# Making the ternary weights of the last layer inside an earlier stage of a two-layer decoder

## The chip, the cores and the metric

The kernel runs on one core of a Trainium2 chip. The metric is the device time of one execution in microseconds (us), measured from outside the program; a profiled execution also has a span, from its first to its last instruction. Engines are named as in the profile: PE (TensorE matmuls), PEld (its weight loads), DVE (VectorE), ACT (ScalarE), POOL (GpSimd), SP (SyncE, which here only issues DMAs); SPq and POOLq are DMAs issued from those two engines.

## The reference

Input x is [4, 512, 512]: 2048 tokens of 512. Six blocks follow, each `x = layernorm(x + block(x))`: an 8-wide-head attention, a cross attention on features, a mixture of experts, a causal attention with rotary angles, a cross attention with axial rotary angles, and a gated feed-forward net with ternary weights. Two of them matter here.

- Mixture of experts: eight experts with hidden widths 256 to 1024, the best two for each token, on a latent of 256; a shared expert and a core matrix beside them.
- The ternary net. Its weights are 2048x512, 2048x512 and 512x2048 (4 MB each in float32), and each is quantised with one scale that needs the mean of all its magnitudes first:

```python
def _quant_weight(w):
    scale = jnp.mean(jnp.abs(w)) + EPS
    wq = jnp.clip(jnp.round(w / scale), -1.0, 1.0)
    return (wq, scale)
def _qlinear(x, w):            # activations are rounded to 8 bits with a scale per row
    wq, ws = _quant_weight(w)
    xq, xs = _quant_act(x)
    return jnp.einsum('bsi,oi->bso', xq, wq) * xs * ws
gate = silu(_qlinear(x, w_gate)); up = _qlinear(x, w_up); out = _qlinear(gate * up, w_down)
```

The weights depend on no activation, so they can be made at any time. The net multiplies by their transposes, so that each 128x128 block is also turned.

## The kernel before

The program runs stage after stage; the token array `m.x_tok` stays in SBUF. Each stage is a block in which every engine has its own instruction list, written out in the order of the Python loops; semaphores join the lists, and an engine that waits holds back all that stands behind in its list. All engines meet at the end of a block.

**The experts' items** (`mixture_of_experts`, L629). Tokens are sorted by expert into 24 tiles of 256 tokens, and the work is cut into `ITEMS` = 79 items, each one slice of 256 hidden columns of one expert on one tile. For item i the lists hold:

- SP (L741 to L779): two DMAs of the item's weights, 257 and 256 KB (`load_item`, three slots `item`, so three items ahead); for the first items the rows of a token tile (`load_rows`, 256 KB); every fourth item one `store_tile` (L758), which waits until DVE has added that tile's last item.
- PE (L943): `turn_rows(i + 4)` while there are tiles, `hidden(i + 1)` (8 matmuls, L924), `output(i)` (8 matmuls, L935). The result of `output` goes to one of four banks (`mm`), which DVE empties.
- ACT: the gelu of the hidden columns (L1022) and a copy of the next token tile (L1011).
- DVE (L1213 to L1220): `keep_turned(i + 4)` while there are tiles, then one add of the bank to the accumulator `acc` (L1220).
- POOL: nothing during the items. Its list has the scatter of the token rows, 24 memsets and four adds to x, then the wait `pool.wait_ge(s.stored, SPARE * 16)`, and the gathers that follow the last item.

`w.core` (8 KB a partition) and `w.down` (4 KB) are weights of this stage that are last read before the items.

**The ternary weights** (`ternary_weights`, L2307) are the first block of the last stage, and the token loop (`ternary_ffn`) is its second. SP loads 12 pieces of 1 MB. ACT adds up magnitudes piece by piece (L2367); PE sums them over the partitions (L2418); DVE makes the scale (L2385 to L2389) and then, for each piece, three `tensor_scalar` passes over 128x2048: scale and round (L2394), subtract and cap at 1 (L2400), cap at -1 (L2402). PE turns the blocks, four 128x128 transposes to a bank, four banks to a piece (192 transposes, `turn_tile`, L117), and ACT and DVE copy every other bank to `tf_gate`, `tf_up`, `tf_down` (L2378, L2406). ACT's sums of weight i + 1 are interleaved with the turning of weight i. The order within DVE's list is `for c in range(PARTS + 1)`: quantise piece c, then copy the odd banks of piece c - 1.

Of the kernel before, what the change touches and what calls it, by code (L numbers as in the profile page):

```python
# [21 lines left out]
BF16 = mybir.dt.bfloat16  # L22
# [11 lines left out]
LN_EPS = 1e-5  # L34

# [524 lines left out]
class Packed:  # L560

    def __init__(self, nc, ctx):
        self.items = nc.dram_tensor("moe_items", (PAIR0[EXPERTS], P, PACKED), F32, kind="Internal").ap()
        self.sorted = nc.dram_tensor("moe_sorted", (TILES * TOKENS, LATENT), F32, kind="Internal").ap()
        self.mixed = nc.dram_tensor("moe_mixed", (SPARE * TOKENS, LATENT), F32, kind="Internal").ap()
        self.items_in, self.cleared = ctx.enter_context(nc.semaphore("moe_items_in")), ctx.enter_context(nc.semaphore("moe_cleared"))
# [61 lines left out]
def mixture_of_experts(nc, m, w, packed, a):  # L629
# [10 lines left out]
    LATER = 2  # L640
    EARLY, PAD = 4, T // 2 + 1
    hc_at = numbered([key for b in range(B) for key in [("x", b, j) for j in range(NT)] + [("rows", b - 1, h) for h in range(HALVES) if b > 0]]
                     + [("rows", B - 1, h) for h in range(HALVES)] + [("gates", b) for b in range(B)]
                     + [("turn", n) for n in range(TILES)] + [("sums", t) for t in range(T)])
# [7 lines left out]
    with ExitStack() as ctx:  # L652
# [46 lines left out]
        s.returned_in = [sem(f"returned_in_{i}") for i in range(RETURNED)]  # L699
        s.x_now_ready, s.returned_used = sem("x_now_ready"), sem("returned_used")  # L700
# [81 lines left out]
        def _(pe):  # L782
# [251 lines left out]
        def _(dve):  # L1034
# [173 lines left out]

            dve.wait_ge(s.which_ready, 1)
            for n in range(AHEAD):  # L1210
                keep_turned(n)
            for i in range(ITEMS):
# [7 lines left out]
                dve.tensor_tensor(to, bank(("item", i)), to, ALU.add).then_inc(free(("item", i)), 1)  # L1220

# [36 lines left out]
        def _(pool):  # L1258
# [30 lines left out]
            for b in range(B):  # L1289
                x = m.x_tok[:, b * NT:(b + 1) * NT, :]  # L1290
                pool.tensor_tensor(x, x, w.up_b[:].unsqueeze(1).to_broadcast([P, NT, D]), ALU.add).then_inc(s.x_biased, 1)
            pool.wait_ge(s.stored, SPARE * 16)
# [1008 lines left out]
INNER = 2048  # L2301
KI = INNER // P
QUANT_EPS = 1e-5
ROUND_INT = 1.5 * 2.0 ** 23

def ternary_weights(nc, m, w, w_gate, w_up, w_down):  # L2307

    WEIGHTS, PARTS = 3, 4
    FREE = D * INNER // P
    PIECE = FREE // PARTS
    SLOTS = 6
    LOADS = 3
    with ExitStack() as ctx:
        sb, sem = allocator(nc, ctx, "tw")
        raw = [sb(f"raw{i}", [P, FREE]) for i in range(WEIGHTS)]  # L2320
        quant = sb("quant", [P, SLOTS, PIECE], BF16)
        sums, ones, total, inv = sb("sums", [P, 3, PARTS]), sb("ones", [P, P]), sb("total", [P, 3]), sb("inv", [P, 3])
        ident_b, spare = sb("ident_b", [P, P], BF16), sb("spare", [P, PIECE], BF16)
        loaded = [sem(f"loaded{i}") for i in range(LOADS)]
        made, ident_made, summed, added, scaled, rounded = (sem(n) for n in ("made", "ident_made", "summed", "added", "scaled", "rounded"))
        full = [sem("even_full"), sem("odd_full")]
        free = [sem("even_free"), sem("odd_free")]
        TILES = D * INNER // (P * 4 * P)
        BANKS = TILES // PARTS
        block = ctx.enter_context(nc.Block())  # L2330

        def turned(i, n):

            if i < 2:
# [4 lines left out]
        def piece(i, c):  # L2339
            return raw[i][:, c * PIECE:(c + 1) * PIECE]  # L2340

        def wait_loaded(engine, i, c):
            q = i * PARTS + c
            engine.wait_ge(loaded[q % LOADS], q // LOADS * 16 + 16)

        @block.sync
        def _(sp):
            for i, source in enumerate((w_gate, w_up, w_down)):
                rows = P * PIECE // source.shape[1]
                for c in range(PARTS):  # L2350
                    if i * PARTS + c >= LOADS:
                        q = i * PARTS + c - LOADS
                        wait_loaded(sp, q // PARTS, q % PARTS)
                    sp.dma_start(piece(i, c).rearrange("p (o n) -> p o n", n=source.shape[1]),
                                 source[c * rows:(c + 1) * rows, :].rearrange("(o p) n -> p o n", p=P)) \
# [326 lines left out]
```

## Time and profile before

| | |
|---|---|
| median of 3 runs | 3102.58 us (3102.41 to 3107.42) |
| the profiled execution's own time | 3105.17 us |
| its span | 3103.4 us |
| busy share of the span: PE, DVE, ACT, POOL | 90%, 59%, 45%, 13% |
| experts' items, by DVE's first and last add | 830.1 to 1106.2 us |
| ternary weights block, first DMA issue to last copy | 2789.9 to 2859.6 us |
| DMA | 147.54 MB, mean 48 GB/s |

### The profile page before, as it was taken

What the parts mean: (1) busy time and instruction counts of PE and PEld (TensorE: products, weight loads), DVE (VectorE), ACT (ScalarE), POOL (GpSimd) and SP (SyncE); (2) the same over time, 40 slices, a digit from 0 to 9 for tenths busy, and PEclk for the clock granted to TensorE, in tenths of its full rate; (3) what the DMA queues carried; (4) which work ended last, traced back from release to release, by engine and by line L of the source; (5) the groups of instructions that cost most, each with busy time, mean ns of one, the idle gap of its engine ahead of it and who ended that gap; (6) DMA issues with size and microseconds to landing.
All of it is one profiled execution on the core that took longest, in us unless ns stands there. A gap on an engine that the chain in (4) does not pass through costs nothing. (4 is left out here: it accounts for less than half of the span.)

```text
span 3103.4 us, 40349 instructions
## 1 busy us (share of the span) xinstructions
PE 2781.8 (90%) x12377; PEld 1644.4 (53%) x12400; DVE 1839.6 (59%) x3505; ACT 1394.6 (45%) x2964; POOL 398.8 (13%) x437
## 2 busy tenths in 40 slices
PE   8999996889999976998998998996999999983887
PEld 4455453344688845655655655654555454433333
DVE  5666563524222155756756756753777777746776
ACT  4454442121133412543542642542667676745544
POOL 0310003003300041102102102102010101000010
PEclk9999998999899998999999999998999999995999
DMA  3390007002366634000000000001000000004000
GB/s 129 49 100 14 14 0 247 29 1 75 94 193 172 171 102 156 1 1 15 1 1 15 1 1 14 1 1 55 8 2 9 2 5 2 2 8 157 7 20 27
DMA packets 74599, 147.54 MB, mean 48 GB/s; under 512 B 11136, under 2 KB 27537, under 8 KB 71985
## 3 DMA queue, kind: packets, MB, share of 16 engines
q1 hardware_dynamic: 62976, 111.53, 11.2%
q0 software_dynamic: 11440, 33.77, 5.8%
q8 instruction: 91, 1.49, 0.2%
q14 instruction: 92, 0.75, 0.1%
HBM read 112.50 MB, written 31.22 MB: 46 GB/s over the span
## 5 line engine op out<-in xcount | busy, mean ns | idle before, releaser
L2207 DVE TENSOR_REDUCE x_neg_max<-bank 128x1 f32<-128x512 f32 x512 | 327.2, 684 | 96.1 <-PE bank L2052 95.5
L2159 ACT ACTIVATE x_weights<-bank 128x512 f32<-128x512 f32 x512 | 279.1, 600 | 127.1 <-PE bank L2063 122.3
L1507 PE MATMUL bank<-a_wo,a_att_cols 128*128 128x512 f32 x512 | 226.9, 594 | 7.8 <-DVE a_q_cols L1607 4.1
L1557 ACT ACTIVATE a_probs<-bank,a_neg_max 128x128 f32<-128x128 f32 (+3 forms) x256 | 138.4, 540 | 192.5 <-DVE a_neg_max L1655 192.2
L117 PE MATMUL bank<-all_ident,a_probs 128*128 128x128 f32 x1216 | 197.0, 275 | 16.3 <-DMA a_probs<-all_x_tok 16.3
L117 PEld LDWEIGHTS bank<-all_ident,a_probs 128*128 128x128 f32 x1216 | 155.3, 142 | 104.4 <-issue 52.5
L1549 ACT COPY a_probs_t<-bank 128x128 f32<-128x128 f32 (+3 forms) x256 | 108.7, 424 | 193.7 <-PE bank L117 193.7
L1220 DVE TENSOR_TENSOR moe_acc<-bank,moe_acc 128x512 f32 x79 | 54.6, 692 | 214.0 <-PE bank L935 214.0
L1482 PE MATMUL bank<-a_k_cols,a_q_cols 128*128 128x128 f32 (+3 forms) x512 | 176.8, 434 | 0.0
L1448 PE MATMUL bank<-a_x_high,a_w_high 128*128 128x512 f32 x320 | 137.3, 429 | 38.6 <-DVE a_q_cols L1607 12.9
L1686 POOL TENSOR_TENSOR a_w_low<-a_wqkv,a_w_high 128x512 fp32r<-128x512 f32 x64 | 81.4, 1272 | 591.0 <-ACT a_w_high L1520 591.0
L1507 PEld LDWEIGHTS bank<-a_wo,a_att_cols 128*128 128x128 f32 x512 | 94.2, 190 | 113.4 <-issue 106.0
L924 PE MATMUL bank<-moe_gh_cols,moe_item 128*128 128x256 f32 x632 | 151.2, 382 | 0.4 <-issue 0.4
L935 PE MATMUL bank<-moe_item,moe_wide 128*128 128x256 f32 x632 | 149.4, 379 | 0.0
L1494 PE MATMUL bank<-a_probs_t,a_v_rows 128*128 128x512 f32 (+3 forms) x512 | 148.6, 433 | 0.0
L1563 ACT ACTIVATE a_probs<-a_probs,a_inv_sum 128x128 f32<-128x128 f32 (+3 forms) x256 | 144.8, 566 | 2.5 <-DVE a_inv_sum L1660 2.5
L1022 ACT ACTIVATE moe_wide<-bank,moe_item 128x256 f32<-128x256 f32 x158 | 66.3, 470 | 166.5 <-PE bank L924 166.5
L2052 PE MATMUL bank<-x_k_cols,x_q_cols 64*128 64x512 f32 x512 | 136.4, 496 | 3.5 <-DVE x_neg_max L2207 3.4
L1629 DVE TENSOR_TENSOR all_x_tok<-bank,all_x_tok 128x512 f32 (+1 forms) x64 | 44.2, 691 | 158.6 <-PE bank L1507 158.6
L1655 DVE TENSOR_REDUCE a_neg_max<-bank 128x1 f32<-128x128 f32 (+3 forms) x256 | 125.7, 491 | 20.9 <-issue 2.6
L2085 PE MATMUL bank<-x_weights,x_v_rows 128*17 128x512 f32 x1024 | 134.5, 598 | 0.0
L2063 PE MATMUL bank<-x_q_cols,x_k_cols 64*128 64x512 f32 x512 | 127.6, 415 | 3.2 <-ACT x_weights L2159 2.8
(402 smaller groups left out, 5714.1 us busy)
## 6 DMA issues: line engine op xcount, KB each, us to landing
moe_item<-moe_items SPq DMA_DIRECT2D x79, 257.0 KB, 3.0
moe_item<-moe_items SPq DMA_DIRECT2D x79, 256.0 KB, 3.2
moe_items<-in_L_ffn_e_w POOLq DMA_DIRECT2D x40, 256.0 KB, 35.3
moe_sorted<-x_zeros POOLq DMA_DIRECT2D x1, 6144.0 KB, 22.8
moe_x_cols<-moe_sorted SPq DMA_DIRECT2D x24, 256.0 KB, 3.6
moe_mixed<-moe_acc SPq DMA_DIRECT2D x23, 256.0 KB, 3.3
all_x_tok<-in_x SPq DMA_DIRECT2D x1, 4096.0 KB, 17.7
x_x_rows<-all_x_tok SPq DMA_DIRECT2D x4, 1024.0 KB, 9.1
```

What stands on the lines that cost most here:

```text
L117: last = pe.transpose(bank[:, c * P:(c + 1) * P], rows[:, c * P:(c + 1) * P], ident)
L924: last = pe.matmul(bank(("hidden", i))[:, c * TOKENS:(c + 1) * TOKENS], weight[:, k, c * P:(c + 1) * P], x_now[:, i % 2, k * TOKENS:(k + 1 ...
L935: last = pe.matmul(bank(("item", i))[:, j * LATENT:(j + 1) * LATENT], hid[:, i % 2, c * TOKENS + j * P:c * TOKENS + (j + 1) * P], weight[: ...
L1448: last = pe.matmul(mm[g % 2], weight[:, p % 2, k, :], x[:, k, :], start=n == 0, stop=n == 3 * KD - 1)
L1482: pe.matmul(sc[n % 4][:, 0:t], q_cols[:, h % 2, j * P:t], k_cols[:, h // GROUP, 0:t], start=True, stop=True).then_inc(s.sc.full, 1)
L1494: last = pe.matmul(mm[g % 2][:, c * P:], v_rows[:, c, kv * HD1:(kv + 1) * HD1], probs_t[:, n % 2, c, c * P:], start=c == 0, stop=c == NT - 1)
L1507: last = pe.matmul(mm[g % 2], att_cols[:, h % HALF_HEADS, j * P:(j + 1) * P], wo[:, h, :], start=h == first, stop=h == end - 1)
L1557: act.activation(probs[:, n % SLOTS, 0:t], sc[n % 4][:, 0:t], ACT.Exp, bias=neg_max[:, n:n + 1], accum_out=row_sum[:, n:n + 1]).then_inc(s ...
L1563: act.activation(probs[:, i % SLOTS, 0:t1], probs[:, i % SLOTS, 0:t1], ACT.Copy, scale=inv_sum[:, i:i + 1]).then_inc(s.probs_ready, 1)
L2052: pe.matmul(score_banks[slot % 3], q_cols[rows, u % 2, pair, j * P:(j + 1) * P], k_cols[rows, u % 2, pair, :], start=True, stop=True).then ...
L2159: act.activation(weights[:, chunk % 2, k, :], weight_banks[slot % 2], ACT.Exp).then_inc(s.weight.free, 1)
L2207: dve.tensor_reduce(neg_max[:, g % 2, j, h:h + 1], score_banks[slot % 3], AX.X, ALU.max, negate=True) \
```

## The change

The three weights are made ternary during items 12 to 63 and written to a DRAM tensor `packed.ternary` in bf16; the last stage loads that tensor (6 MB instead of 12) and only turns it. Each weight is cut into eight pieces of 128x1024 (512 KB in float32, 256 KB in bf16), 24 in all, in two buffers over `w.core` (raw) and two over `w.down` (ternary).

- Items 12 to 35: after each item's add, DVE sums the magnitudes of one piece, with one `tensor_reduce`.
- Item 38: PE sums over the partitions, one small matmul. Item 39: DVE makes the three scales.
- Items 40 to 63: after each item's add, DVE makes one piece ternary, in the same three passes as before. The pieces are loaded from DRAM a second time.
- POOL issues all of these DMAs, in one loop that stands ahead of its wait for `s.stored`: 24 loads for the sums, and 24 loads and 24 stores for the ternary round. Load q + 2 waits until DVE is done with piece q.
- The last stage's first block has 12 loads of 512 KB (six ahead), 192 transposes over all eight banks, and the copies, shared out between ACT and DVE as before. No sum, no scale and no quantising pass is left in it.

```diff
@@ mixture_of_experts
+    EIGHTHS_ALL = WEIGHTS * EIGHTHS
+    SUM_AT, SCALE_AT = 12, 12 + EIGHTHS_ALL + 2
+    QUANT_AT = SCALE_AT + 2
...
+        raw = w.core[:].rearrange("p k n -> p (k n)").rearrange("p (i n) -> p i n", i=2)
+        ternary = w.down[:].rearrange("p k n -> p (k n)").bitcast(BF16).rearrange("p (i n) -> p i n", i=2)
...
@@ tensor
+                if i == SCALE_AT:
+                    pe.wait_ge(s.abs_summed, EIGHTHS_ALL)
+                    pe.wait_ge(*room("scale"))
+                    pe.matmul(bank("scale")[:, 0:EIGHTHS_ALL], ones[:], abs_sum[:].rearrange("p i g -> p (i g)"),
+                              start=True, stop=True).then_inc(full("scale"), 1)
@@ vector
+            def add_magnitudes(q):
+                dve.wait_ge(s.raw_in[q % 2], (q // 2 + 1) * 16)
+                dve.tensor_reduce(abs_sum[:, q // EIGHTHS, q % EIGHTHS:q % EIGHTHS + 1], raw[:, q % 2, :], AX.X, ALU.add,
+                                  apply_absolute_value=True).then_inc(s.abs_summed, 1)
...
+            def make_ternary(q):
+                slot, i = q % 2, q // EIGHTHS
+                dve.wait_ge(s.raw_in[slot], (EIGHTHS_ALL // 2 + q // 2 + 1) * 16)
+                dve.tensor_scalar(raw[:, slot, :], raw[:, slot, :], inv_scale[:, i:i + 1], ROUND_INT, ALU.mult, ALU.add)
+                dve.drain()
+                if q >= 2:
+                    dve.wait_ge(s.ternary_out[slot], q // 2 * 16)
+                dve.tensor_scalar(ternary[:, slot, :], raw[:, slot, :], ROUND_INT, 1.0, ALU.subtract, ALU.min)
+                dve.drain()
+                dve.tensor_scalar(ternary[:, slot, :], ternary[:, slot, :], -1.0, None, ALU.max).then_inc(s.ternary_ready, 1)
...
                 dve.tensor_tensor(to, bank(("item", i)), to, ALU.add).then_inc(free(("item", i)), 1)
+                if SUM_AT <= i < SUM_AT + EIGHTHS_ALL:
+                    add_magnitudes(i - SUM_AT)
+                if i == SCALE_AT + 1:
+                    weight_scales()
+                if QUANT_AT <= i < QUANT_AT + EIGHTHS_ALL:
+                    make_ternary(i - QUANT_AT)
@@ gpsimd
+            for n in range(2 * EIGHTHS_ALL + 2):
+                q = n - 2
+                if 0 <= q < EIGHTHS_ALL:
+                    pool.wait_ge(s.abs_summed, q + 1)
+                elif q >= EIGHTHS_ALL:
+                    q -= EIGHTHS_ALL
+                    pool.wait_ge(s.ternary_ready, q + 1)
+                    pool.dma_start(packed.ternary[q // EIGHTHS, q % EIGHTHS], ternary[:, q % 2, :]).then_inc(s.ternary_out[q % 2], 16)
+                if n < 2 * EIGHTHS_ALL:
+                    load_raw(n)
...
             pool.wait_ge(s.stored, SPARE * 16)
@@ ternary_weights
-            for i, source in enumerate((w_gate, w_up, w_down)):
...
+            for q in range(PIECES):
+                if q >= LOADS:
+                    sp.wait_ge(loaded[q % LOADS], q // LOADS * 16)
+                i, c = divmod(q, PARTS)
+                sp.dma_start(quant[:, q, :].rearrange("p (g n) -> p g n", g=2),
+                             packed.ternary[i, 2 * c:2 * c + 2].rearrange("g p n -> p g n")).then_inc(loaded[q % LOADS], 16)
...
+            for n in range(0, WEIGHTS * TILES, 2):
+                act.wait_ge(full[0], n // 2 + 1)
+                act.copy(turned(n), blocks_of(bank(n), 4)).then_inc(free[0], 1)
...
+            for n in range(1, WEIGHTS * TILES, 2):
+                dve.wait_ge(full[1], n // 2 + 1)
+                dve.tensor_copy(turned(n), blocks_of(bank(n), 4)).then_inc(free[1], 1)
...
+            for n in range(WEIGHTS * TILES):
+                q, part = divmod(n, BANKS)
+                if part == 0:
+                    pe.wait_ge(loaded[q % LOADS], q // LOADS * 16 + 16)
+                pe.wait_ge(free[n % 2], n // 2 + 1)
+                turn_tile(pe, bank(n), quant[:, q, part * 4 * P:(part + 1) * 4 * P], ident_b[:], 4).then_inc(full[n % 2], 1)
```

The order of DVE's list in the later items, before: `moe_which` holds each item's tile number, and `moe_acc<-bank,moe_acc` is the add.

```order
497 L1215 TENSOR_LOAD moe_which
498 L1215 ISA x2
499 L1220 ISA
500 L1220 TENSOR_TENSOR moe_acc<-bank,moe_acc 128x512
501 L1215 TENSOR_LOAD moe_which
```

And in the changed kernel at items 40 and 41: `ew_core` is the raw piece, `ew_down` the ternary one.

```order
546 L1266 TENSOR_TENSOR moe_acc<-bank,moe_acc 128x512
547 L1247 TENSOR_SCALAR ew_core<-ew_core,moe_inv_scale 128x1024
548 L1251 TENSOR_SCALAR ew_down<-ew_core 128x1024
549 L1253 TENSOR_SCALAR ew_down<-ew_down 128x1024
550 L1261 TENSOR_LOAD moe_which
551 L1261 ISA x2
552 L1266 ISA
553 L1266 TENSOR_TENSOR moe_acc<-bank,moe_acc 128x512
```

Three passes, and the wait for the piece ahead of the first, now stand between one item's add and the next one's.

POOL's list from the adds to x to the gathers, before:

```order
178 L1288 MEMSET moe_acc 128x512 x24
179 L1291 TENSOR_TENSOR all_x_tok<-all_x_tok,ew_up_b 128x2048 x4
180 L1299 DMA moe_x_cols<-moe_mixed,moe_index 128x256 x18
```

And in the changed kernel, its beginning (the last two rows then repeat):

```order
179 L1343 TENSOR_TENSOR all_x_tok<-all_x_tok,ew_up_b 128x2048 x4
180 L1354 DMA ew_core<-in_L_ffn_w_gate 128x2x512 x8
181 L1354 DMA ew_core<-in_L_ffn_w_up 128x2x512 x8
182 L1354 DMA ew_core<-in_L_ffn_w_down 128x1024 x8
183 L1354 DMA ew_core<-in_L_ffn_w_gate 128x2x512 x2
184 L1363 DMA ternary<-ew_down 128x1024
185 L1354 DMA ew_core<-in_L_ffn_w_gate 128x2x512
```

The 72 new DMAs stand between the adds to x and the gathers; in the second round a store and a load follow one another.

## Rows read from the trace of the kernel before

**Rows 1.** The page, busy time of each engine over the span.
```profile
PE 2781.8 (90%) x12377; PEld 1644.4 (53%) x12400; DVE 1839.6 (59%) x3505; ACT 1394.6 (45%) x2964; POOL 398.8 (13%) x437
```

**Rows 2.** Windows: us, busy of PE, PEld, DVE, ACT, POOL, PE clock, DMA share, GB/s.
```profile
870.00:890.00 20.00, 20.00 (x104) 17.61 (x103) 6.75 (x11) 6.78 (x15) 0.00 (x0) 1.00 0.74 216
950.00:970.00 20.00, 20.00 (x95) 17.58 (x94) 3.75 (x6) 8.32 (x18) 0.00 (x0) 1.00 0.64 184
2800.00:2810.00 10.00, 0.56 (x2) 0.50 (x2) 3.14 (x6) 6.20 (x8) 0.00 (x0) 0.50 1.05 390
2830.00:2840.00 10.00, 4.41 (x39) 3.86 (x39) 9.48 (x14) 8.46 (x11) 0.00 (x0) 0.50 0.00 1
```

**Rows 3.** DVE's add in the items, by its line: duration, idle before it by releaser.
```profile
L1220 DVE TENSOR_TENSOR moe_acc<-bank,moe_acc x79: 690/692/693, 830.1 to 1106.2; 128x512 f32 x79
  PE bank L935: 214.0, 79
```

**Rows 4.** Timeline of one item's add: start, us, engine, line, names, count, idle before.
```profile
935.16 0.69 DVE L1220 TENSOR_TENSOR moe_acc<-bank,moe_acc 128x512 f32 x1 [2.77 <-PE bank L935]
```

**Rows 5.** Timeline of the ternary block, its start, one piece, its end.
```profile
2789.93 5.88 SPq L2354 DMA_DIRECT2D tw_raw<-in_L_ffn_w_gate  x4
...
2795.52 1.91 ACT L2367 ACTIVATE tw_spare<-tw_raw 128x2048 bf16<-128x2048 f32 x1 [24.48 <-DMA tw_raw<-in_L_ffn_w_gate]
...
2828.78 0.58 ACT L2378 COPY tf_up<-bank 128x512 bf16<-128x512 bf16 x1 [2.88 <-PE bank L117]
...
2829.64 0.58 ACT L2378 COPY tf_up<-bank 128x512 bf16<-128x512 bf16 x1 [0.27 <-PE bank L117]
...
2859.13 0.42 DVE L2406 COPY tf_down<-bank 128x512 bf16<-128x512 bf16 x1 [0.43 <-PE bank L117]
```

**Rows 6.** Groups by line, 2740 to 2880: busy us, mean ns, idle before.
```profile
L2367 ACT ACTIVATE tw_spare<-tw_raw 128x2048 bf16<-128x2048 f32 x12 | 22.9, 1910 | 27.9 <-DMA tw_raw<-in_L_ffn_w_gate 26.7 <-DMA tw_raw<-in_L_ffn_w_up 0.7
L2394 DVE TENSOR_SCALAR tw_raw<-tw_raw,tw_inv 128x2048 f32<-128x2048 f32 x12 | 15.4, 1279 | 0.3
L2400 DVE TENSOR_SCALAR tw_quant<-tw_raw 128x2048 bf16<-128x2048 f32 x12 | 14.7, 1227 | 1.3
L2402 DVE TENSOR_SCALAR tw_quant<-tw_quant 128x2048 bf16<-128x2048 bf16 x12 | 8.3, 694 | 0.9
L2604 DVE TENSOR_REDUCE tf_top_h<-tf_inner 128x1 f32<-128x2048 f32 x1 | 2.3, 2287 | 0.1
L2588 DVE TENSOR_SCALAR tf_shifted_x<-all_x_tok,tf_inv_x 128x512 f32<-128x512 f32 x3 | 1.5, 486 | 0.2
```

**Rows 7.** DMA issues: count, KB each, median us from issue to landing.
```profile
moe_item<-moe_items SPq DMA_DIRECT2D x79, 257.0 KB, 3.0
...
ew_core<-in_L_ffn_core_w POOLq DMA_DIRECT2D x1, 1024.0 KB, 11.7
...
ew_down<-in_L_ffn_down_w POOLq DMA_DIRECT2D x1, 512.0 KB, 4.6
...
moe_sorted<-moe_acc,moe_index POOLq DMA_INDIRECT x32, 2.4
```

**Rows 8.** Timelines of POOL and DVE (129 on), columns as in rows 4.
```profile
128.96 0.98 POOL L579 DMA_DIRECT2D moe_items<-in_L_ffn_e_w  x1
129.04 2.02 DVE L97 TENSOR_SCALAR all_x_tok<-all_x_tok,a_ln_mean_var,a_ln_rstd  x4 [1.15 <-POOL a_ln_rstd L104]
...
131.42 0.69 POOL L579 DMA_DIRECT2D moe_items<-in_L_ffn_e_w  x1
```

**Rows 9.** Timeline of PE at the items' start, turning rows, then matmuls.
```profile
817.40 4.00 PE L913 MATMUL bank<-all_ident,moe_x_cols 128*128 128x128 f32 x16
...
821.78 3.75 PE L924 MATMUL bank<-moe_gh_cols,moe_item 128*128 128x256 f32 x8 [0.38 <-issue]
```

**Rows 10.** Windows there, columns as in rows 2.
```profile
821.00:822.00 1.00, 0.62 (x3) 0.25 (x3) 0.84 (x2) 0.67 (x2) 0.00 (x0) 0.50 0.84 273
...
826.00:827.00 1.00, 1.00 (x7) 0.90 (x6) 0.69 (x1) 0.99 (x2) 0.00 (x0) 1.00 0.19 20
```

More of the change, by code:

```diff
@@ L643, in mixture_of_experts @@
                      + [("rows", B - 1, h) for h in range(HALVES)] + [("gates", b) for b in range(B)]
-                     + [("turn", n) for n in range(TILES)] + [("sums", t) for t in range(T)])
+                     + [("turn", n) for n in range(TILES)] + ["scale"] + [("sums", t) for t in range(T)])
     lg_at = numbered([(kind, b) for b in range(B) for kind in ("router", "logits")] + ["rank", "const", "sum"]
@@ L2337, in turned, with bank @@
             return w.down[:, 4 * q:4 * q + 4, o * P:(o + 1) * P]
[L2339 to L2344, printed above, removed]
+        def bank(n):
+            return m.banks[n % 8].bitcast(BF16)
         @block.sync
         def _(sp):
-            for i, source in enumerate((w_gate, w_up, w_down)):
[L2349 to L2355, printed above, removed]
-                      .then_inc(loaded[(i * PARTS + c) % LOADS], 16)
@@ L2363, in _ @@
         def _(act):
-            def add_up(i, c):
-                wait_loaded(act, i, c)
-                act.drain()
-                act.activation(spare[:], piece(i, c), ACT.Abs, accum_out=sums[:, i, c:c + 1]).then_inc(summed, 1)
-            for c in range(PARTS):
-                add_up(0, c)
-            for i in range(WEIGHTS):
-                for c in range(PARTS):
-                    if i + 1 < WEIGHTS:
-                        add_up(i + 1, c)
-                    for n in range(c * BANKS, (c + 1) * BANKS, 2):
-                        g = i * TILES // 2 + n // 2
-                        act.wait_ge(full[0], g + 1)
-                        act.copy(turned(i, n), blocks_of(m.banks[2 + g % 2].bitcast(BF16), 4)).then_inc(free[0], 1)
+            for n in range(0, WEIGHTS * TILES, 2):
+                act.wait_ge(full[0], n // 2 + 1)
+                act.copy(turned(n), blocks_of(bank(n), 4)).then_inc(free[0], 1)
@@ L2408, in _ @@
+            for n in range(1, WEIGHTS * TILES, 2):
+                dve.wait_ge(full[1], n // 2 + 1)
+                dve.tensor_copy(turned(n), blocks_of(bank(n), 4)).then_inc(free[1], 1)
         @block.tensor
         def _(pe):
[L2410 to L2412 removed]
+            pe.sem_inc(free[0], 4)
+            pe.sem_inc(free[1], 4)
             pe.wait_ge(ident_made, 1)
[L2414 to L2426 removed]
```

110 lines of the change are left out of this document (45 added, 65 removed).

## The prediction

> **What bounds the kernel now.** I read the page first: PE is busy for 90% of the span, so work taken from any other engine pays only where PE waits [rows 1]. The table of windows shows two stretches that the change touches and that are opposites. In the items PE is busy for all of 20 us out of 20 at the full clock, while DVE works for 3.75 to 6.75 us and POOL not at all; the DMA share is 0.64 to 0.74. In the ternary block PE is busy for 0.56 and 4.41 us out of 10, at a granted clock of 0.50, and the busiest engine is first the DMA (390 GB/s, share 1.05), then DVE (9.48 of 10) [rows 2]. The reader is to see in the first an engine that nothing may delay, and in the second a block that DMA and DVE set.
>
> Next the line of DVE's add: 79 adds of 692 ns, with 214.0 us of idle time before them, all ended by PE. DVE waits for PE, never the reverse [rows 3]. One of them shows the item's length: 2.77 us idle and 0.69 of add, 3.46 us [rows 4]. That is the cover for the moved work.
>
> Last the ternary block itself: first DMA issue at 2789.93, first sum at 2795.52, last copy from 2859.13 to 2859.55 [rows 5]. It lasts 69.6 us, and nothing else runs beside it.
>
> **The ternary block, what goes and what is left.** The 12 sums on ACT (22.9 us) and DVE's three passes over 12 pieces (15.4 + 14.7 + 8.3 = 38.4 us) go [rows 6]. Left are 12 loads of 0.5 MB, 192 transposes and 48 copies; what is late next is found by the rate of each.
> - DMA: 524 KB at 390 GB/s is 1.34 us a piece [rows 2]. The first 1 MB piece was used 5.6 us after its issue, of which 2.7 is transfer [rows 5]; a half piece saves 1.3. So the first piece is there at 2795.5 - 1.3 = 2794.2, the last at 2794.2 + 11 x 1.34 = 2808.9.
> - PE at the clock of this block: ACT copies every other bank, and two of its copies with PE as releaser start 0.86 us apart (2828.78, 2829.64), so a bank takes 0.43 us and a piece of four banks 1.72 [rows 5].
> - ACT: two copies a piece, 0.58 us each, 1.2 us. DVE's take 0.42 each [rows 5].
>
> PE is the slowest of them: 12 x 1.72 = 20.6 us from 2794.2 is 2814.8, and the last copy ends 0.7 later, 2815.5. Against 2859.55 that saves 44.0 us. It rests on the half clock. PE has nothing to turn before the first piece is there, in either kernel, so it starts at 0.50. Would gapless transposes lift it? At the items' start 16 transposes ran for 4.00 us without a gap (817.40) and the clock was still 0.50 after them; then eight matmuls ran 3.75 us from 821.78, and at 826 it was 1.00 [rows 9, 10]. I therefore leave it at half.
>
> The Trainium skill says the same in "TensorE: Matmul & The Clock Gate", Part 4: the full level does not engage for transposes, since they don't count as a busy PE in the same way. Its Part 1 would have them counted as sustained activity like matmuls; which of the two holds for twenty microseconds of them, no run here shows yet.
>
> With the full clock from 2801 on, DMA would be the slowest: last piece at 2808.9, turned and copied about 2 us later, 2811. That saves 48.5 us, and is the upper end of this term. The lower end is 42, if the half-size loads reach only nine tenths of the rate.
>
> **The items, what is added to DVE.** The shapes are new (128x1024), the operations not. A pass over 2048 takes 1279 ns and over 512 takes 486 [rows 6], so over 1024 by the line through both 750, of which 220 is there at any size. With half of the slope part and this fixed part the three passes take 0.75 + 0.72 + 0.46 = 1.9 us, with drains 2.0. The sum over 2048 takes 2287 ns (`tf_top_h`) [rows 6], over 1024 about 1.25. Against 2.77 us of idle time per item both fit, with 0.77 us left in the ternary round and 1.5 in the sums' round; in the first 20 items DVE also copies turned tiles, and is busy for 6.75 us in 20 instead of 3.75 [rows 2]: the 13 us left in 20 hold five sums of 1.25. So the arithmetic costs nothing as long as the piece is there when DVE comes to it. The matmul for the scales and its wait: 0.3 us; the three tiny DVE operations 0.5 us, hidden.
>
> **The items, the wait that is added.** DVE now waits for a DMA between two adds. Behind that wait stands the next item's add, behind the add the bank that PE needs four items later, and SP's `store_tile`, behind which the next item's weights stand. A slot is reloaded only when DVE is done with it, so two items must hold one whole round trip. For the ternary round: 2.0 (passes) + 0.1 + 0.7 (POOL issues the store) + landing of the load. For the sums' round: 1.25 + 0.1 + landing. The trace has no load of this kind in this place, so I bound the landing from both sides. An indirect DMA of 128 KB from POOL lands 2.4 us after its issue [rows 7]; less 0.34 of transfer that is 2.06 fixed, plus 1.34 for our size 3.4. The one load of our size from POOL, `ew_down`, took 4.6 [rows 7]. Beside it come the item loads, which hold the queues: the share of 0.64 [rows 2] leaves 0.36, and a transfer of 1.34 beside half-busy engines takes 2.0 to 2.7, so 4.1 to 6.0 in all. An upper end comes from a load that queued behind others, `ew_core` with 11.7 [rows 7].
> - Sums' round: 1.35 + 4.1 to 6.0 = 5.5 to 7.4 us for two items of at least 6.9. No cost, up to 5 us; I take 1.
> - Ternary round: 2.8 + 4.1 to 6.0 = 6.9 to 8.8 us, 3.45 to 4.4 an item against 3.46. Times 24 items: 0 to 23 us. DVE may fall behind PE by one to two items before PE (four banks) or SP's store feels it, which absorbs some 5 us. So 0 to 18; I take 7, for 3.95 us an item.
>
> By bytes the ternary round wants 513 + 512 + 256 KB an item and a fourth of 256 for the tile stores, 1.38 MB in 3.46 us or 398 GB/s. The highest rate in these rows is 390 [rows 2]. That is why I don't take zero.
>
> The item loads themselves (3.0 us to landing [rows 7]) are issued up to three items, 10.4 us, ahead of use, so they can double without reaching PE. 72 more issues on POOL at 0.7 us [rows 8] lie in its idle stretch, and the loop ends near item 66, before the wait for `s.stored` opens.
>
> One rule speaks against the change. What the rows show: with four DVE passes from SBUF to SBUF running beside it (129.04), POOL's issue took 0.98 us, and 0.69 two us later [rows 8]. So an overlap costs POOL about 0.3 us, and I have it within the range.
>
> The Trainium skill, "SBUF — State Buffer", on the trap that DVE blocks DMA, says that a DVE operation in a two-port mode locks GpSimd out, so that no descriptors of a POOL DMA are written until it ends. By that rule each of the two issues per item could wait for a whole pass of 0.75 us, 1.5 us in the round trip; the sum would then lose 24 x 0.75 = 18 us more, and still end faster than before.
>
> **The sum.** Profiled execution 3105.2 - 44.0 (block) + 7 (ternary round) + 1 (sums' round) + 0.3 (scale matmul) = 3069.5. The median of the runs shown stands 2.6 us below that execution (3102.6 against 3105.2), so I forecast 3067 us.
>
> **Rivals.**
> - A, the clock rises in the turning block. For: PE has no gaps there, unlike before, when it was busy for 4.41 us in 10 [rows 2]. Against: rows 9 and 10 as read above. The block then saves 48.5, and the time is 3062.5; if besides the round trips are all hidden, 3054.
> - B, the ternary round is bound by its round trip much more than I take, 4.6 us an item, through the port lock or both streams at 398 GB/s: 24 x 1.14 - 5 = 22, so 15 more than forecast, 3082. For: the byte count; against: PE-side slack and the share of 0.64.
> - C, slower than before: POOL's loads queue as `ew_core` did, because each load stands behind a store and behind the item loads in every DMA engine. With a landing of 11.7 the ternary round takes (2.8 + 11.7) / 2 = 7.25 us an item and the sums' round 6.5, against 3.46 and about 3.6. Less 5 each, that is 86 + 65 = 151 us, and the time is 3102.6 - 44 + 151 = 3210. It decides from a landing of 7.3 us on, where both rounds together lose the 44 (ternary 5.05, sums 4.3 an item: 38 + 17 - 10 = 45). Against: `ew_core` stood behind 1 MB of earlier loads of its own queue; here at most one store of 256 KB does.
> - D, the change doesn't do what it says: some pass or sum would still run in the last block. The listing of instructions shows none, so I give it nothing.
>
> **How the numbers follow.** Forecast with its own range of 3058 to 3077: 0.68. A with hidden round trips, below 3058: 0.10. B: 0.16. C: 0.06. The range holds the time 8 times in 10 when it reaches from 3054 to 3083: it leaves out C and a few in a hundred on either side. A measurement of this kernel tells 0.2% (6 us) from no change. Faster needs less than 3096: the forecast, A, B and the mild end of C, 0.95. Same 0.02, slower 0.03.
>
> **What the new profile would show.** Right if: the items' adds span 276 + 5 to 15 us; in items 40 to 63 DVE's first pass has idle time before it with the load as releaser, and in items 12 to 35 the sum has next to none; PE idle in the items is a few us; the last block has 24 + 24 copies, a clock of 0.50 and a length of 24 to 28 us. The size of the turning term is wrong if the clock there is 1.00. Wrong in the main if PE's idle time in the items passes 44 us, or if the first piece of the last block lands much later than 4.3 us after its issue.

## The result, and the profile after

The changed kernel takes 3089.09 us (median of 6 runs, 3077.00 to 3098.03), the kernel before 3103.74 beside it: a ratio of 0.9951, 95% interval 0.9931 to 0.9971. So 15 us came where 36 were forecast. The profiled execution took 3098.03 us, the slowest of the six, with a span of 3096.3.

The span by stages, read from DVE's adds (items), SP's first DMA (later blocks) and POOL's first instruction (token loop), in the profiled executions:

| stage | before | after | difference | forecast |
|---|---|---|---|---|
| up to the first add | 830.1 | 832.3 | +2.2 | 0 |
| items 0 to 12 | 46.7 | 46.7 | 0.0 | 0 |
| items 12 to 36 (sums) | 86.0 | 89.9 | +3.9 | +1 |
| items 36 to 40 (scales) | 13.8 | 14.9 | +1.0 | +0.3 |
| items 40 to 64 (ternary) | 82.9 | 111.0 | +28.1 | +7 with the next row |
| items 64 to 78 | 46.7 | 43.6 | -3.0 | |
| last add to fourth block | 70.2 | 68.9 | -1.3 | 0 |
| fourth block (causal attention) | 949.8 | 952.1 | +2.4 | 0 |
| fifth block (rotary cross attention) | 663.8 | 669.6 | +5.8 | 0 |
| ternary weights block | 69.9 | 21.7 | -48.2 | -44.0 |
| token loop | 243.6 | 245.7 | +2.1 | 0 |
| sum | 3103.4 | 3096.3 | -7.1 | -35.7 |

First the page, in answer to [rows 1]:

```profile
PE 2794.7 (90%) x12396; PEld 1649.4 (53%) x12396; DVE 1878.6 (61%) x3559; ACT 1371.0 (44%) x2940; POOL 443.8 (14%) x508
```

DVE is busier, not idler: moving work doesn't remove it, and each weight is now cut into smaller passes.

The items 40 to 64 as windows (the columns of [rows 2]), a stretch of before for comparison, then after:

```profile
962.80:1045.70 82.90, 82.90 (x385) 72.91 (x384) 16.60 (x24) 33.27 (x72) 0.00 (x0) 1.00 0.61 172
```
```profile
984.40:1095.40 111.00, 94.48 (x413) 80.25 (x412) 61.91 (x97) 35.72 (x78) 27.53 (x46) 0.95 0.91 299
```

PE, busy for every microsecond before, is idle for 16.5 of 111, and its clock is at 0.95 instead of 1.00. What DVE does there, by line (columns as in [rows 6]), answers to [rows 3]:

```profile
L1247 DVE TENSOR_SCALAR ew_core<-ew_core,moe_inv_scale 128x1024 f32<-128x1024 f32 x24 | 19.0, 790 | 32.9 <-DMA ew_core<-in_L_ffn_w_up 12.1 <-DMA ew_core<-in_L_ffn_w_down 11.4 <-DMA ew_core<-in_L_ffn_w_gate 9.4
L1266 DVE TENSOR_TENSOR moe_acc<-bank,moe_acc 128x512 f32 x25 | 17.3, 692 | 14.7 <-issue 10.9 <-PE bank L950 3.8
L1251 DVE TENSOR_SCALAR ew_down<-ew_core 128x1024 bf16<-128x1024 f32 x24 | 16.9, 703 | 1.8
L1253 DVE TENSOR_SCALAR ew_down<-ew_down 128x1024 bf16<-128x1024 bf16 x24 | 10.3, 427 | 1.8
```

Before, every add waited for PE. Now the add waits for PE for 3.8 us, and the first pass waits for the raw piece for 32.9. PE's own waits there have one row (wait, total, times, longest):

```profile
PE bank L939 <- DMA moe_item<-moe_items: 16.5, 7, 6.0
```

It names a DMA of item weights, which lands 1.6 us later than before at the median; but SP issues it behind a `store_tile` that waits for DVE. The landings in that stretch, after, answer to [rows 7]:

```profile
moe_item<-moe_items SPq DMA_DIRECT2D x26, 257.0 KB, 4.6
ternary<-ew_down POOLq DMA_DIRECT2D x24, 256.0 KB, 4.4
ew_core<-in_L_ffn_w_up POOLq DMA_DIRECT2D x8, 512.0 KB, 6.1
ew_core<-in_L_ffn_w_down POOLq DMA_DIRECT2D x8, 512.0 KB, 6.2
ew_core<-in_L_ffn_w_gate POOLq DMA_DIRECT2D x6, 512.0 KB, 7.0
```

The ternary block (against [rows 5]) and its windows:

```profile
2828.96 6.91 SPq L2412 DMA_DIRECT2D tw_quant<-ternary  x9
2832.64 3.57 PE L123 MATMUL bank<-tw_ident_b,tw_quant 128*128 128x128 bf16 x32 [8.99 <-DMA tw_quant<-ternary]
...
2848.81 1.07 PE L123 MATMUL bank<-tw_ident_b,tw_quant 128*128 128x128 bf16 x16 [0.22 <-DMA tw_quant<-ternary]
...
2849.47 0.87 DVE L2426 COPY tf_down<-bank 128x512 bf16<-128x512 bf16 x2 [0.41 <-PE bank L123]
```
```profile
2834.00:2839.00 5.00, 5.00 (x54) 5.00 (x53) 2.50 (x7) 3.55 (x7) 0.00 (x0) 0.55 1.04 389
2839.00:2844.00 5.00, 3.71 (x61) 3.20 (x59) 3.13 (x8) 3.77 (x8) 0.00 (x0) 1.00 1.05 387
```

PE starts at 0.50 and turns without a gap; the clock is 0.55 in the first window shown and 1.00 in the second. A piece of 16 transposes then takes 1.07 us, and PE waits for DMA, whose share is 1.05 at 387 GB/s: rival A's picture.

### The profile page after: what moved, and what is told of

Same layout as the page of the kernel before. It is cut to its first block and busy times, and to the rows that moved or that the text cites. A ratio compares the mean times of both kernels' runs of the same rounds, so it can differ in the third digit from the quotient of the medians.

```text
span 3096.3 us, 40464 instructions
## 1 busy us (share of the span) xinstructions
PE 2794.7 (90%) x12396; PEld 1649.4 (53%) x12396; DVE 1878.6 (61%) x3559; ACT 1371.0 (44%) x2940; POOL 443.8 (14%) x508
## 3 DMA queue, kind: packets, MB, share of 16 engines
q8 instruction: 91, 1.49, 0.2%
## 5 line engine op out<-in xcount | busy, mean ns | idle before, releaser
L939 PE MATMUL bank<-moe_gh_cols,moe_item 128*128 128x256 f32 x632 | 157.9, 395 | 20.2 <-DMA moe_item<-moe_items 19.7
L939 PEld LDWEIGHTS bank<-moe_gh_cols,moe_item 128*128 128x128 f32 x632 | 121.5, 197 | 41.6 <-DMA moe_item<-moe_items 24.9
L950 PEld LDWEIGHTS bank<-moe_item,moe_wide 128*128 128x128 f32 x632 | 121.9, 193 | 17.3 <-issue 0.3
```

The source lines that it names most:

```text
L939: last = pe.matmul(bank(("hidden", i))[:, c * TOKENS:(c + 1) * TOKENS], weight[:, k, c * P:(c + 1) * P], x_now[:, i % 2, k * TOKENS:(k + 1 ...
L950: last = pe.matmul(bank(("item", i))[:, j * LATENT:(j + 1) * LATENT], hid[:, i % 2, c * TOKENS + j * P:c * TOKENS + (j + 1) * P], weight[: ...
```

## The experiments

Kernels of one group ran on one chip, beside runs of the kernel before. The groups differ by 1.2% (medians of before 3103 to 3139 us; 0.4% between the second and the fourth, which have the same chip number), so ratios are compared across groups, and stage times from profiles: before has 86.0 us in items 12 to 36 and 82.9 in 40 to 64 in every profile of it. Theory 1 is the round trip through two buffers, theory 2 the bytes, theory 3 DVE's own work and POOL's descriptors beside it.

**First group** (before 3134.3 us). Four raw buffers in the ternary round, the two new ones over `x_cols`:

```diff
-                dve.wait_ge(s.raw_in[slot], (EIGHTHS_ALL // 2 + q // 2 + 1) * 16)
+                piece = raw_again(q)          # (raw, raw, more, more)[q % 4]
+                dve.wait_ge(s.again_in[q % 4], ...)
```

> Four buffers for the raw pieces of the ternary round instead of two (the two more lie over the token rows' buffers, free by then); bytes, passes and their places in DVE's list are as in the changed kernel. Theory 1, the round trip of a buffer: DVE's 32.9 us of waits for raw loads in the ternary round come from two items having to hold 2.0 us of passes, two issues and a landing of 6 us or more; with four items for it they go, items 40 to 64 take 83 to 87 us instead of 111, and the time is 3060 to 3066. Theory 2, the DMA engines are full: 1.38 MB an item at the 300 GB/s that were delivered is 4.5 us an item whatever the buffers, the round stays at 105 to 111 us, and the time at 3084 to 3090.

The load ahead of the store in POOL's list, released by the second pass:

```diff
+                        pool.wait_ge(s.raw_free, q + 1)
+                        load_raw(n)
                     pool.wait_ge(s.ternary_ready, q + 1)
                     pool.dma_start(packed.ternary[...], ternary[:, q % 2, :])
```

> POOL issues the next raw load as soon as DVE's second pass has read the buffer, ahead of the store, instead of after the third pass and the store. Theory 1: the round trip is shorter by 0.5 (third pass) and 0.6 us (store issue) of some 8.9, so 3.9 us an item instead of 4.6, round of 94 to 100 us, time 3071 to 3078. Theory 2: the bytes are the same, no change, 3084 to 3090.

No second loads:

```diff
-                dve.wait_ge(s.raw_in[slot], (EIGHTHS_ALL // 2 + q // 2 + 1) * 16)
...
-                if n < 2 * EIGHTHS_ALL:
+                if n < EIGHTHS_ALL:
                     load_raw(n)
```

> The second round of loads is left out; DVE makes ternary what lies in the buffers (so the weights are not the right ones), all passes and stores stay. Theories 1 and 2: the round takes 83 to 84 us, time 3060 to 3064. Theory 3, DVE itself is full (passes 2.0, add 0.69 and 0.47 us to read the item's tile number, 3.16 of 3.46 us, and each pass longer when POOL writes descriptors): the round stays above 88 us even without loads, time over 3068.

The ternary round spread over items 40 to 74:

```diff
-                if QUANT_AT <= i < QUANT_AT + EIGHTHS_ALL:
+                if i in QUANT_ITEMS:          # [40 + q * 3 // 2 for q in range(24)]
```

> The 24 pieces are made ternary in items 40 to 74, two in every three items, instead of 40 to 63; two buffers, store and load order as in the changed kernel. Theory 1: three items, 10.4 us, hold a round trip of 8.9, so there is no wait left: items 40 to 78 take 131 to 135 us, as before the change (129.6), time 3060 to 3066. Theory 2: 1.09 MB an item are wanted in 3.46 us, 315 GB/s, just about the rate that was delivered, so some of the loss stays, 3064 to 3075. Theory 3 gives 3060 to 3066 as well.

Measured (us; the ratio with its 95% interval):

| | ratio to before | items 40 to 64 | 64 to 78 |
|---|---|---|---|
| four buffers | 0.9921 [0.9908, 0.9933] | 94.2 | 46.6 |
| load first | 0.9920 [0.9906, 0.9935] | 98.9 | 46.6 |
| no second loads | 0.9873 [0.9859, 0.9888] | 82.9 | 46.6 |
| spread | 0.9913 [0.9900, 0.9925] | 89.0 | 49.1 |

Without the second loads the round takes exactly what it took before the change, though DVE still has all three passes, and POOL all 24 stores, in it: theory 3 falls for these; POOL's issues of the loads went with the loads. With the load first, a round trip shorter by about 1.1 us takes 12.1 us off the round, which ends in the 94 to 100 us that theory 1 expected. With four buffers DVE never waits for a raw piece, and 16.9 of the 28.1 us are gone: theory 1 holds for that part, but not for all, as it expected 83 to 87 us. Of the 11.3 us left, PE is idle for 8.0, nearly all of it (7.9) waiting for item weights, now without a late DVE behind them, and its 385 matmuls take 3.2 us more than before, at a clock of 1.00 in both kernels. PE's waits of this kernel over all items, and the window of items 40 to 64:

```profile
PE bank L946 <- DMA moe_item<-moe_items: 12.5, 15, 1.7
```
```profile
1009.58:1103.74 94.16, 86.12 (x385) 71.93 (x384) 59.39 (x96) 33.01 (x72) 26.45 (x44) 1.00 0.94 327
```

The spread kernel takes 138.1 us from item 40 to 78, where theory 1 expected 131 to 135 and before has 129.6; DVE waits 0.2 us for a raw piece in its items 40 to 64. That part of the loss, 8.5 us, is not the round trip.

**Second group** (before 3114.3 us). The changed kernel again, unchanged:

> The changed kernel once more, beside the others on one chip. Both theories: its ratio to the kernel before is the first one, 0.993 to 0.997; items 40 to 64 take 108 to 113 us, 12 to 36 take 89 to 92. If the parts between the experts and the last stage are longer by 8 us again, that is part of the change and not of the one execution.

`store_tile` three items later in SP's list:

```diff
-                if (stored + 1) * max(PAIRS) + SLOTS <= i:
+                if (stored + 1) * max(PAIRS) + SLOTS + 3 <= i:
```

> SP issues each tile store three items later than in the changed kernel; nothing else. Theory 1a, the coupling through SP's list: an item's weights stand behind a store that waits for a DVE that lags, so PE's waits for moe_item (16.5 us in the ternary round) come from there and go; DVE's own waits stay, so the round falls from 111 to 98 to 104 us. Theory 1b, DVE is the chain and PE's waits only mirror it: the round stays at 108 to 113 us.

Four buffers, and only half of each raw piece loaded in the ternary round:

```diff
-    pool.dma_start(raw_again(q).rearrange("p (o n) -> p o n", n=D), weight_rows(q))
+    pool.dma_start(raw_again(q)[:, 0:D], weight_rows(q)[:, 0, :])
```

> As the kernel with four buffers, but each load of the ternary round brings only half of its piece (256 KB; so half of the weights are stale). Count of DMAs, passes and waits are the same. With four buffers the ternary round took 94.2 us, 11 more than without the change, with PE waiting for moe_item. Theory 2, bytes in the DMA engines: 1.12 MB an item instead of 1.38, the round falls to 83 to 87 us. Theory 4, the number of DMAs or POOL's descriptor work holds back the item loads: the round stays at 91 to 95 us.

Four buffers, and both rounds spread:

```diff
-    SUM_AT, SCALE_AT = 12, 12 + EIGHTHS_ALL + 2
+    SUM_ITEMS = [1 + q * 5 // 4 for q in range(EIGHTHS_ALL)]      # 1 to 29
+    QUANT_ITEMS = [34 + q * 15 // 8 for q in range(EIGHTHS_ALL)]  # 34 to 77
```

> Both rounds are spread: sums at items 1 to 29, five pieces in six items, ternary round at items 34 to 77, with four buffers. 0.8 to 1.0 MB an item. Theories 1 and 2 together: no wait for raw pieces in DVE's list, PE waits for moe_item below 5 us, all items take 276 to 281 us (before 276.1), and the time is the kernel's before less 40 to 45 us, a ratio of 0.986 to 0.988. If it stays above 0.990, something else than round trip and bytes costs the rest.

| | ratio to before | items 12 to 36 | 40 to 64 | 64 to 78 |
|---|---|---|---|---|
| changed again | 0.9946 [0.9929, 0.9962] | 91.2 | 111.0 | 42.4 |
| store late | 0.9935 [0.9921, 0.9949] | 90.5 | 111.2 | 35.9 |
| four buffers, half pieces | 0.9887 [0.9868, 0.9905] | 91.5 | 85.9 | 46.6 |
| both spread, four buffers | 0.9914 [0.9899, 0.9930] | 89.4 | 87.9 | 49.0 |

The late store is the instructive one. PE's waits change their name, and the round keeps its length. In all items of that kernel:

```profile
PE bank L950 <- DVE moe_acc L1266: 9.2, 9, 2.1
PE bank L939 <- DMA moe_item<-moe_items: 7.5, 7, 2.1
```

DVE is the chain, whichever list passes its delay on to PE. Nor is it PE's clock that makes the round long. The window of items 40 to 64 of this kernel has a clock of 1.00, that of the changed kernel 0.95, and both take 111 us:

```profile
991.84:1103.02 111.18, 98.22 (x439) 81.71 (x437) 61.39 (x97) 38.49 (x84) 27.53 (x46) 1.00 0.92 307
```
 What changed is the end: with a longer backlog of banks, PE gets back 6.5 us more after item 64, but the ratio moved by 0.1%, within its interval.

Half the bytes with the same number of DMAs takes the round from 94.2 to 85.9: of the 11.3 us left by four buffers, 8.3 go with the bytes. Theory 2 holds for that part, with one reserve: the packets in the round fall with the bytes, from 13255 to 12037, so the two aren't told apart. 3.0 us stay.

Both rounds spread over four buffers missed their expectation. The items take 290.5 us where 276 to 281 were expected, and PE waits 8.7 us for item weights where less than 5 were. DVE waits for no raw piece. So spreading takes off the round trip, and about half of the 30 us stays beside the item loads: PE's waits, and 4.2 us by which its matmuls take longer (280.1 us busy against 275.9).

**Third group** (before 3110.3 us). The kernel before, twice, the changed one, and both rounds spread with the two buffers of the change (the diff of the last one, without the four buffers):

> The kernel before, unchanged, for its stage times on the chip of the other kernels of this job. Theory A (the untouched stages are longer because of what the changed kernel does, its DRAM tensor, its code or its queues): the fourth block (causal attention) takes 949 to 951 us and the fifth (cross attention with rotary angles) 663 to 664, as in the first profile of before, in every profile. Theory B (these differences are the chip's and the execution's own): the fifth block takes 665 to 668 us here too, and the fourth 951 to 954. Ratio to before 1.000 in either case, within 0.2%.

> The same kernel once more, for the spread of its stage times between two profiled executions on one chip. Theory A: the two profiles agree within 1 us in each of the two attention blocks, both at the lower values. Theory B: they differ by 1 to 3 us.

> The changed kernel, unchanged, beside the two profiles of before on the same chip. Theory A: fourth block 2 us and fifth block 3 to 6 us longer than in both profiles of before here; items 40 to 63 111 us; the first block of the last stage 21.7 us, the last token loop 2.0 us longer than in before. Theory B: the two attention blocks are as long as in before within 1 us; the other three numbers the same. Ratio to before 0.995 in either case.

> Both rounds spread out (24 sums over items 1 to 29, 24 ternary pieces over items 34 to 77, about every second item), with the two buffers of the changed kernel. Theory 1 (the round trip with two buffers): at one piece in 1.9 items a slot has 13 us for its round trip of 9.2, so DVE has no wait for raw pieces left, and two buffers are as good as four: items 290 us as in the version with four buffers, ratio 0.990 to 0.992. Theory 2 (bytes): the same, since the bytes per microsecond are the same as there; PE keeps 8 to 15 us of waits for item weights. A rival (four buffers are needed even so, since loads queue behind item loads for more than 13 us): items over 298 us, ratio 0.994 or more.

| | ratio to before | fourth block | fifth block | all items |
|---|---|---|---|---|
| before again | 0.9997 [0.9985, 1.0009] | 949.8 | 663.6 | 276.1 |
| before, third | one run | 951.8 | 663.8 | 276.1 |
| changed, third | 0.9942 [0.9924, 0.9959] | 950.5 | 670.4 | 304.9 |
| both spread, two buffers | 0.9908 [0.9892, 0.9925] | 953.1 | 670.3 | 292.2 |

Spread, two buffers are as good as four: DVE waits for no raw piece in the ternary round and 1.6 us in the sums' round, and PE waits 9.5 us for item weights. With 3082.43 us (3081.80 to 3083.31) it is 10 us faster than the changed kernel beside it (3090.26 to 3097.37); from the spread and the four-buffer kernels, at 0.9913 to 0.9921, it can't be told apart. The changed kernel's fourth block lies between the two of before. Its fifth is longer by 6.6 us, so in this group the fifth block spoke for theory A of its expectations, and the fourth for theory B.

**Fourth group** (before 3103.1 us): each half of the change alone, and the changed kernel without any load.

```diff
 # items only: the last stage makes its own weights, as before
-        ternary_weights(nc, m, w, packed)
+        ternary_weights(nc, m, w, w_gate, w_up, w_down)
```

> One half of the change alone: the items make the ternary weights and store them, as in the changed kernel, and the last stage ignores them and makes its own, as before. Theory A1 (the work in the items, or the instructions added there, lengthens the fifth block): fifth block 666 to 670 us, last stage as before (69.9 and 243.6); items 306 us; ratio to before 1.010 to 1.013 (30 us of items, 3 to 6 of the fifth block). Theory A2 (the new last stage, its tensor or its place in memory does it): fifth block 663.7; ratio 1.009 to 1.010.

```diff
 # last block only: no loads, sums or scales in the items
-                dve.tensor_scalar(...)   # three passes
+                dve.memset(ternary[:, slot, :], 1.0).then_inc(s.ternary_ready, 1)
```

> The other half alone: the new first block of the last stage, with the 24 stores of 256 KB in items 40 to 63, but no loads, no sums and no quantising in the items (DVE writes ones into the pieces, so the weights are not the reference's). Items 276 us by every theory, since nothing is waited for; the first block of the last stage 21.7 us, the token loop 2.0 us longer. Theory A1: fifth block 663.7, so the time falls by 48.2 - 2.0 = 46 us: ratio 0.985 to 0.986. Theory A2: fifth block 666 to 670, ratio 0.986 to 0.988.

```diff
 # no loads: POOL's loop keeps the 24 stores alone
-                if n < 2 * EIGHTHS_ALL:
-                    load_raw(n)
```

> The changed kernel without any of the 48 loads: sums, scales, the three passes and the 24 stores stay, on weights that lie in SBUF (so the result is not the reference's). Theory of the loads (all of the 30 us in the items comes from loads, as waits of DVE or as bytes beside the item weights): items 276 to 277 us, of which items 12 to 36 take 86.0 and items 40 to 64 take 82.9. Rival (DVE's sums and the scale step cost by themselves): items 12 to 40 take 4 to 5 us more than the 99.8 of before. Ratio to before 0.985 to 0.987 by the first, 0.988 by the second.

| | ratio to before | items 12 to 40 | 40 to 64 | all items | fifth block | ternary block |
|---|---|---|---|---|---|---|
| items only | 1.0100 [1.0065, 1.0134] | 104.8 | 110.0 | 301.7 | 667.8 | 70.3 |
| last block only | 0.9862 [0.9832, 0.9891] | 99.8 | 82.9 | 276.1 | 672.8 | 21.7 |
| no loads | 0.9861 [0.9829, 0.9893] | 100.1 | 83.5 | 276.9 | 670.1 | 21.7 |

The halves add up: +1.0% and -1.4%. Without the loads all sums, scales, passes and stores cost 0.8 us in 79 items, so nearly all of the 30 us is the loads, in the sums' round too. The windows of the whole items, without loads and (both spread, two buffers) with them:

```profile
825.81:1102.72 276.91, 276.34 (x1316) 242.42 (x1314) 135.49 (x196) 105.64 (x229) 13.08 (x24) 1.00 0.66 200
```
```profile
829.22:1121.38 292.16, 280.78 (x1316) 241.21 (x1314) 135.89 (x197) 106.14 (x229) 43.01 (x70) 1.00 0.86 271
```

**Fifth group** (before 3138.9 us). Each half alone has a longer fifth block than before has in its three profiles, none of which was taken in that group. Instructions and waits there are those of before. What differs is the time that PE takes for the block's 3616 matmuls, 627.3 us in before and 634.2 after, and with it the granted clock, as in 12 matmuls of the same kind 26 to 28 us into the block. Timeline and window of before, then of after:

```profile
2152.46 2.82 PE L2033 MATMUL bank<-x_wkv,x_c_cols 128*128 128x256 f32 x12
...
2152.40:2155.40 3.00, 2.88 (x15) 2.22 (x13) 0.87 (x2) 1.53 (x2) 1.14 (x1) 1.00 0.00 0
```
```profile
2187.73 5.45 PE L2109 MATMUL bank<-x_wkv,x_c_cols 128*128 128x256 f32 x12
...
2187.70:2193.20 5.50, 5.50 (x15) 3.97 (x14) 1.52 (x4) 1.53 (x2) 1.27 (x1) 0.50 0.00 0
```

The same 12 matmuls take 2.82 us at a clock of 1.00 and 5.45 at 0.50. In the 4 us ahead of them PE is idle for over half of the time in both kernels, busy for 1.84 us before (2148.15 to 2152.15) and 1.49 after (2183.37 to 2187.37), and only in the second does the clock fall. Both kernels of this group are the kernel before with one unused allocation:

```diff
+        m.scale = sb("scale", [P, 3])                                            # the first
+        self.ternary = nc.dram_tensor("ternary", (3, 8, P, 1024), BF16, ...)     # the second
```

> The kernel before with one more SBUF allocation, 12 bytes a partition beside the token array, as the changed kernel has it, and never used; every later buffer lies 12 bytes (or its rounding) further on. Placement in SBUF as the cause: fifth block 666 to 672 us, ratio 1.001 to 1.003. Any other cause: 663.7 us, ratio 1.000.

> The kernel before with one more DRAM tensor of 6 MB that is never used. Placement in DRAM as the cause: fifth block 666 to 672 us. Any other cause, the history of load before the block included: 663.7 us.

The first has 0.9993 [0.9978, 1.0009] and a fifth block of 666.6 us; the second, one run, 667.3. So the block also takes 3 to 4 us more where neither the items' work nor the new last block exists. The chip of this group is 0.9% slower than the one of the third, and the plain kernel was not profiled on it, so that allocation and chip can't be told apart; the ratio of the first kernel, 0.9993, shows no longer time, where placement as the cause expected 1.001 to 1.003. The changed kernel itself has 669.6, 666.7 and 670.4 us in its three profiles. "Theory A" of the third group is not shown by this: what sets the dips stays open.

## Why the prediction was off, point by point

- **What bounds it**: right. PE has the items, and DMA with DVE had the ternary block.
- **The ternary block**: the direction right, the size off by 4 us because its step "I therefore leave it at half" failed. The clock did not stay at 0.50 through a gapless run of transposes: it stood at 1.00 from 2839 to 2844. From [rows 9, 10] I had taken that the matmuls raised it there and the 16 transposes ahead of them had no part in it; the rows could not tell that. By the rule in the Trainium skill, "TensorE: Matmul & The Clock Gate", Part 4, the level should not have risen; this case goes with Part 1 of that page, as the prediction reads it. The priced alternative, 48.5 us, is what came (48.2).
- **The arithmetic in the items**: right that it costs nothing (0.8 us with all loads away), but the slack was mis-sized. The forecast gave DVE 0.77 us to spare in the ternary round. One cycle of the changed kernel:

```profile
1016.85 0.75 DVE L1247 TENSOR_SCALAR ew_core<-ew_core,moe_inv_scale 128x1024 f32<-128x1024 f32 x1 [1.91 <-DMA ew_core<-in_L_ffn_w_gate]
1017.68 0.69 DVE L1251 TENSOR_SCALAR ew_down<-ew_core 128x1024 bf16<-128x1024 f32 x1
1018.45 0.43 DVE L1253 TENSOR_SCALAR ew_down<-ew_down 128x1024 bf16<-128x1024 bf16 x1
1019.34 0.69 DVE L1266 TENSOR_TENSOR moe_acc<-bank,moe_acc 128x512 f32 x1 [0.46 <-issue]
1020.82 0.75 DVE L1247 TENSOR_SCALAR ew_core<-ew_core,moe_inv_scale 128x1024 f32<-128x1024 f32 x1 [0.79 <-DMA ew_core<-in_L_ffn_w_up]
```

  From the first pass to the end of the add is 3.18 us of 3.46. In the 0.46 labelled "issue" DVE's list has nothing but the read of the item's tile number (`TENSOR_LOAD`) and the instructions that go with it, so I put the time down to that read; no run takes it away. The list of before has it too, but hidden under the wait for PE, so that no row showed it. With 0.28 us of slack an item, a late piece is hardly ever caught up.
- **The ternary round, +7 forecast, 25 measured**: this is the step that failed, and the largest error. The mechanism, a round trip that two items must hold, was right; its landing was mis-sized. 4.1 to 6.0 us were taken (5.1 for the 7 us), 6.1 to 7.0 measured. The sum for two items is then 2.8 + 6.1 to 7.0 = 8.9 to 9.8 us, 4.4 to 4.9 an item; measured 111.0 / 24 = 4.62. The prediction's own row said more than it took: a share of 0.64 leaves 0.36, and 1.34 us of transfer at that rate is 3.7, with the fixed 2.06 a landing of 5.8. It worked with half-busy engines instead, and without what its own loads and stores add: the share in the round is 0.91. That is rival B, which had 4.6 us and 22 in all, for the round trip and the bytes; the port lock has its own point below. The runs split the 28.1 us: 16.9 for the two-buffer round trip, 8.3 for bytes beside the item weights, 3.0 left, whose cause stays open.
- **The sums' round and the scales, +1.3 forecast, 5 measured**: "no cost" was wrong although the round trip was right, 1.35 + 5.7 to 6.0 = 7.1 to 7.4 us in the forecast's 5.5 to 7.4; what was wrong was to take 1 from its "up to 5". Without loads 0.3 us are left of it, so the rest is again the loads: DVE waits 18.5 us for raw pieces there, most of it covered.
- **The coupling**: right. DVE falls behind, SP's `store_tile` holds the item weights, PE stops; and 3.0 us of backlog came back after item 64, where 5 were taken.
- **POOL beside DVE**: right that it is small, but not because the two got on side by side. In the changed kernel's ternary round none of POOL's 24 store issues and only 8 of its 22 load issues overlap one of DVE's three passes; the others lie behind the third pass and beside the add. Of the eight none takes over 0.71 us. Of the eight passes that begin inside one, six take longer, up to 1.02 us instead of 0.74, 1.2 us in all:

```profile
1011.29 0.70 POOL L1354 DMA_DIRECT2D ew_core<-in_L_ffn_w_gate  x1
1011.50 1.02 DVE L1247 TENSOR_SCALAR ew_core<-ew_core,moe_inv_scale 128x1024 f32<-128x1024 f32 x1
```

  With four buffers one issue took 0.94 us beside a pass (1060.96), where its like take 0.53. By the Trainium skill, "SBUF — State Buffer", on the trap that DVE blocks DMA, a POOL DMA can wait for a whole pass, which the forecast priced at 18 us more. With so few issues beside a pass, this kernel doesn't put that rule to the test.
- **What the sum did not have**: fifth block +5.8 us (2.9 and 6.6 in the other two profiles of the changed kernel, against 663.8), and +2.0 in the token loop, which every kernel with the new last block shows (245.5 to 245.8 against 242.3 to 243.8) and none with the old one; its cause stays open. Other differences of stages lie in the spread of one kernel.

- **Its signs**: DVE's first pass waits for the load, as written. The others fail. The adds span 306.1 us where 276 + 5 to 15 were named, the sum waits 18.5 us for its pieces instead of next to nothing, PE is idle in the items for 20 us instead of a few, and the last block has a clock of 1.00 and 21.4 us to its last copy instead of 0.50 and 24 to 28.

Put together: -48.2 + 30.0 (items) + 2.1 + 5.8, and 3.2 of spread elsewhere, is -7.1 us for this execution. The medians are 14.6 apart because it was the slowest of its six, 8.9 us above their median.

## What to carry to other kernels

Cover is not counted in one engine's idle time alone. A piece that goes through two buffers needs its whole round trip, landing included, within two periods, and a landing read where the queues are half empty is too short for a place where they will be at 0.9. Fewer pieces per period, spread over all of the cover, did as much here as more buffers, for no space at all; but neither brought back more than about half of the 30 us, since the bytes stay beside the loads that PE needs. And when an engine's wait becomes shorter, look for what it had hidden: here half a microsecond in each item, at the place of a register read.

## What had not been expected of the hardware

- The granted clock rose from 0.50 to 1.00 with nothing but transposes on PE: 0.50 in 2829 to 2834, 0.55 in 2834 to 2839, 1.00 in 2839 to 2844.
- Loads of 512 KB that took 4.6 us for one alone [rows 7] take 6.1 to 7.6 with the share at 0.91 to 0.94, and the rates there are 299 to 327 GB/s, not at the 390 of [rows 2].
- Twelve equal matmuls took 2.82 us in one kernel and 5.45 in the other in an untouched block, at clocks of 1.00 and 0.50. Differences of 3 to 7 us in such a block belong to no edit until a control shows them.
